# All matmul operands of a graph-attention kernel as f16 pairs, and four tiles a group transposed by DMA

## The reference

```
h = max(layernorm(x), 0)
q, k, v = h Wq^T, h Wk^T, h Wv^T + bv          (12 heads of 32)
p = softmax(q k^T * 384^-0.5 + 2 adj)           (rows of zeros give 0)
x = x + (p v) Wo^T + bo

h = max(layernorm(x), 0)
for l in 0, 1:
    u_left, u_right = h (h W_left^T)^T, h (h W_right^T)^T   (both / sqrt(384))
    e = exp(u_left above and on adj's diagonal, u_right below) * adj
    h = relu(norm(e / (sum e + 1e-10) (h W_lin^T + b_lin)) * ln_a + ln_b)
x = x + h
```

## Time and profile before

| | |
|---|---|
| median of 3 runs | 1509.78 us (1506.74 to 1509.90) |
| profiled execution | 1507.34 us, its span 1505.4 us |
| mean granted TensorE clock | 0.977 of 2.4 GHz |
| PE busy | 1432.3 us, 95% of the span, 14464 matmuls |
| DVE busy | 1243.8 us, 83% |
| ACT busy | 903.5 us, 60% |
| POOL busy | 508.9 us, 34% |
| HBM | 23.86 MB read, 12.58 MB written |

### The profile page before, as it was taken

One profiled execution on the slowest core, in us unless ns is written; L12 is line 12 of the kernel. 1 busy time (PEld: TensorE's weight loads), 2 busy tenths in 40 slices (PEclk: granted clock), 3 DMA queues, 4 the chain that ended last, 5 costly groups with the idle time before them and its releaser, 6 DMA issues.

```text
span 1505.4 us, 40241 instructions
## 1 busy us (share of the span) xinstructions
PE 1432.3 (95%) x14464; PEld 1396.4 (93%) x14464; DVE 1243.8 (83%) x4619; ACT 903.5 (60%) x2027; POOL 508.9 (34%) x921
## 2 busy tenths in 40 slices
PE   3699999999999999999999999999999999999874
PEld 3599999999999999999999999999999999999874
DVE  5578988888888888888888888888888888888853
ACT  4566665656666556666565666656666665566531
POOL 4113333233334233343323333333333342333321
PEclk8799999999999999999999999999999999999996
DMA  6232322223221223232222333222223222232200
GB/s 216 54 57 58 68 42 62 48 64 68 57 62 43 55 60 64 58 67 50 55 50 61 68 57 68 41 57 53 64 68 57 56 49 57 58 64 57 54 12 11
DMA packets 235683, 89.39 MB, mean 59 GB/s; under 512 B 206784, under 2 KB 235200, under 8 KB 235488
## 3 DMA queue, kind: packets, MB, share of 16 engines
q1 hardware_dynamic: 234912, 85.63, 26.9%
q0 software_dynamic: 576, 1.18, 0.3%
HBM read 23.86 MB, written 12.58 MB: 24 GB/s over the span
## 4 chain that ended last, share of the span: by engine, by line
PE 92%; DVE 2%; DMA 2%; ACT 1%; issue 1%; POOL 1%; SPq 0%; DVEq 0%; POOLq 0%; ACTq 0%
PE bank L342 79%; PE bank L348 4%; PE bank L415 4%; PE bank L403 3%; PE bank L422 1%; DMA x_sb<-x 1%; DMA pT<-prob_parts 1%; PE bank L434 0%; ACT prob L507 0%; SPq L323 0%; DVE weights L570 0%; ACT xn L490 0%; DVE stats_ln L598 0%; ACT prob_parts L515 0%; ACT work L556 0%
## 5 line engine op out<-in xcount | busy, mean ns | idle before, releaser
L342 PE MATMUL bank<-h,weights 128*128 128x256 f32 x3456 | 425.1, 280 | 3.0 <-DVE h L750 3.0
L342 PEld LDWEIGHTS bank<-h,weights 128*128 128x128 f32 x3456 | 411.9, 190 | 3.8 <-issue 3.7
L507 ACT ACTIVATE prob<-prob,rmin 128x128 f32<-128x128 f32 x768 | 244.2, 393 | 3.4 <-DVE rmin L665 3.4
L342 PE MATMUL bank<-weights,h 128*128 128x384 f32 x1152 | 227.5, 342 | 0.0
L342 PE MATMUL bank<-hA,weights 128*128 128x256 f32 x1728 | 219.2, 283 | 1.4 <-DVE hA L585 1.4
L342 PEld LDWEIGHTS bank<-hA,weights 128*128 128x128 f32 x1728 | 212.1, 190 | 1.7 <-DVE hA L585 1.7
L342 PEld LDWEIGHTS bank<-weights,h 128*128 128x128 f32 x1152 | 194.3, 188 | 6.3
L483 ACT ACTIVATE n<-bank 128x512 fp32r<-128x512 f32 x192 | 113.7, 592 | 141.7 <-PE bank L342 141.0
L800 POOL TENSOR_SCALAR less_mean_gnn<-mv_gnn 128x2 f32<-128x2 f32 x64 | 32.9, 513 | 429.9 <-DVE mv_gnn L590 429.9
L665 DVE CUSTOM_DVE_ANT_0 prob<-bank,adj_sb 128x128 f32<-128x128 f32 x768 | 171.0, 286 | 0.2 <-issue 0.2
L585 DVE TENSOR_TENSOR n<-bank,n 128x512 fp32r<-128x512 f32 x192 | 128.9, 684 | 33.8 <-ACT n L483 28.9
(11 more groups left out here) (101 smaller groups left out, 2453.8 us busy)
## 6 DMA issues: line engine op xcount, KB each, us to landing
x_sb<-x SPq DMA_DIRECT2D x32, 384.0 KB, 3.2
out<-x SPq DMA_DIRECT2D x32, 384.0 KB, 2.7
adj_sb<-adj SPq DMA_DIRECT2D x32, 128.0 KB, 2.1
pT<-prob_parts SPq DMA_TRANSPOSE x256, 2.8
x<-w SPq DMA_DIRECT2D x3, 576.0 KB, 4.8
pT<-w SPq DMA_DIRECT2D x3, 576.0 KB, 6.6
prob<-w SPq DMA_DIRECT2D x2, 576.0 KB, 7.3
prob_parts<-w SPq DMA_DIRECT2D x2, 576.0 KB, 6.0
```

What stands on the lines that cost most here:

```text
L342: mm = pe.matmul(out, lhsT, rhs, start=(n == 0), stop=(n == len(pairs) - 1))
L507: e = act.activation(prob[:, a * C + h // HC, :], prob[:, a * C + h // HC, :], ACT.Exp, bias=rmin[:, j, h:h + 1], scale=-1.0)
```

## The change

Each engine's order and the assignment of banks are written anew; the offsets now go from -2 to +1 (before from -1 to +2). Beside that:

- The weights, `hA`, `h0`, `h1`, `oT` and `n2` are f16 pairs. The weights are multiplied by 64 (`W_SCALE`) before the split, and whoever reads the product from PSUM multiplies by 1/64. For VectorE's low parts this makes `scalar_tensor_tensor` of `tensor_tensor`. `dT` and `hl` stay F32R.
- T1a, T1b, OT0, OT1, T2a, T2b, HTa and HTb are gone (24 transposes). In their place come XA, XO, XB and XC: ScalarE copies the rows of the group to a high part, 128 x 768 in f16, VectorE makes the low part, and SP transposes each of the two by one DMA: eight more DMA transposes a group.
- ln_a and ln_b of layer 0 are now applied to rows, by GpSimd (zc0, zc1, zd0, zd1: four operations of 128 x 384), and ScalarE's relu is in the high part of XC.
- `n2`, `hl`, `dT`, `c_sb` exist once for each layer, `mask` and `adjT` once for each of two groups, and layer 0's rows have a tile of their own (`xn2`).
- Seven of the ten weight matrices are staged at once (before four); the other three follow after the step tal.

```diff
-        W = sb("weights", [P, NW, 2, C, H], F32R)
+        W = sb("weights", [P, NW, 2, C, H], F16)
-        hA = sb("hA", [P, 2, C, T], F32R)
+        xa = sb("xn1_parts", [P, 2, G * H], F16)
+        hA = sb("hA", [P, 2, 2, G * C, P], F16)
-        h0 = sb("h0", [P, 2, C, T], F32R)
-        h1 = sb("h1", [P, 2, C, T], F32R)
-        n2 = sb("n2", [P, 2, 2, C, T], F32R)
+        h0 = sb("h0", [P, 2, 2, G * C, P], F16)
+        h1 = sb("h1", [P, 2, 2, G * C, P], F16)
+        n2 = sb("n2", [P, L, 2, 2, C, T], F16)
...
+                elif step in ("tah", "tal", "toh", "tol", "tbh", "tbl", "tch", "tcl"):
+
+                    part, k = "hl".index(step[2]), "X" + step[1].upper()
+                    sp.wait_ge(s_xparts[k][part], g + 1)
+                    for job in USERS[k]:
+                        wait_filled(sp, job, g - 2)
+                    src, dst = {"XA": (xa, hA), "XO": (xo, oT), "XB": (xb, h0), "XC": (xc, h1)}[k]
+                    sp.dma_start_transpose(dst[:, p, part, :, :], src[:, part, :]).then_inc(s_xturned[k][part], 16)
...
-                if step in ("T1a", "T1b"):
-                    for j in range(G):
-                        pe.wait_ge(s_xn1[j], g + 1)
-                    transposes(step, xn1, {"T1a": (0, 1), "T1b": (2,)}[step])
...
+            def split(k, g, rows_in, parts):
+                act.activation(parts[:, HI, :], rows_in.rearrange("p g h -> p (g h)"), ACT.Copy).then_inc(s_xparts[k][HI], 1)
...
+            def split(k, g, rows_in, parts):
+                dve.wait_ge(s_xparts[k][HI], g + 1)
+                ge(dve, s_xturned[k][LO], 16 * g)
+                dve.tensor_tensor(parts[:, LO, :], rows_in.rearrange("p g h -> p (g h)"), parts[:, HI, :], ALU.subtract).then_inc(s_xparts[k][LO], 1)
...
-                dve.tensor_tensor(out, src, hi_part if hi_part.dtype == F16 else hi_part.bitcast(F32), ALU.subtract).then_inc(free(job), 1)
+                dve.scalar_tensor_tensor(out=out, in0=src, scalar=W_BACK, in1=hi_part if hi_part.dtype == F16 else hi_part.bitcast(F32),
+                                         op0=ALU.mult, op1=ALU.subtract).then_inc(free(job), 1)
...
+                elif step[:2] == "zc":
+                    j = int(step[2])
+                    pool.wait_ge(s_z0[j], g + 1)
+                    pool.tensor_tensor(c_sb[:, 0, j, :], c_sb[:, 0, j, :], lna_all[:, 0, :], ALU.mult).then_inc(s_ca[j], 1)
```

SP's order after the change:

```
+        ("tch", -2), ("tcl", -2), ("ld_x", 1), ("pth00", 0), ("tbh", -1), ("tbl", -1), ("pth01", 0), ("ptl01", 0), ("ptl00", 0),
+        ("ld_adj", 1), ("tah", 1), ("tal", 1), ("pth10", 0), ("ptl10", 0), ("pth11", 0), ("ptl11", 0), ("out", -2), ("toh", 0),
+        ("tol", 0)],
```

More of the change, by code:

```diff
@@ L186, in build @@
         wu = work[:, 2 * T:3 * T].rearrange("p (g i) -> p g i", g=G)
[L187 to L191, removed]
+        dT = sb("dT", [P, L, 2, G, P], F32R)
+        c_sb = sb("c_sb", [P, L, G, H])
+        mask = sb("mask", [P, 2, G, 2, P])
+        adjT = sb("adjT", [P, 2, G, P])
         norms = ("ln1", "ln2", "gnn")
@@ L205, in build @@
         carrier = sb("carrier", [P, 4 + G * HC])
-        s_wload = [sem(f"weight_in{i}") for i in range(4)]
+        s_wload = [sem(f"weight_in{i}") for i in range(7)]
         s_setup, s_carrier = sem("setup"), sem("carrier")
@@ L331, in _ @@
                 if g == 0 and step == "ld_x":
-                    load_weights(range(4))
-                if g == 0 and step == "ld_adj":
-                    load_weights(range(4, NW))
+                    load_weights(range(7))
+                if g == 0 and step == "tal":
+                    load_weights(range(7, NW))
             for p in range(2):
@@ L343, in split_mm @@
                 return mm
-            def transposes(job, src, chunks):
-                for n, c in enumerate(chunks):
-                    for j in range(G):
-                        mm = pe.transpose(bank(job)[:, n * T + j * P:n * T + (j + 1) * P], src[:, j, c * P:(c + 1) * P], ident[:, :])
-                mm.then_inc(full(job), 1)
             def need(m, g):
@@ L417, in run @@
                     mm.then_inc(full(step), 1)
-                elif step[:2] == "OT":
-                    j = int(step[2])
-                    wait_drained(pe, f"PV{j}", g)
-                    for c in range(C):
-                        mm = pe.transpose(bank(step)[:, c * P:(c + 1) * P], o_sb[:, j, c * P:(c + 1) * P], ident[:, :])
-                    mm.then_inc(full(step), 1)
-                elif step[:2] == "WO":
-                    wait_drained(pe, f"OT{step[2]}", g)
-                    rows(step, g, WO, oT, 0)
-                elif step in ("T2a", "T2b"):
-                    for j in range(G):
-                        pe.wait_ge(s_xn2[j], g + 1)
-                    transposes(step, o_sb, {"T2a": (0, 1), "T2b": (2,)}[step])
+                elif step[:2] == "WO":
+                    wait_turned(pe, "XO", g)
+                    rows(step, g, WO, oT, int(step[2]))
                 elif step == "AT":
@@ L457, in run @@
                     if g == 0 and l == 0:
-                        pe.wait_ge(s_const, 1)
+                        pe.wait_ge(s_const, L)
                     pe.wait_ge(s_dlo[l], g + 1)
                     wait_drained(pe, f"HL{l}{j}", g)
-                    split_mm(bank(step)[:, 0:HL], [(dT[:, a, j, :], hl[:, b, j, :]) for a, b in PARTS]).then_inc(full(step), 1)
-                elif step in ("HTa", "HTb"):
-                    for j in range(G):
-                        pe.wait_ge(s_z0[j], g + 1)
-                    transposes(step, c_sb, {"HTa": (0, 1), "HTb": (2,)}[step])
+                    split_mm(bank(step)[:, 0:HL], [(dT[:, l, a, j, :], hl[:, l, b, j, :]) for a, b in PARTS]).then_inc(full(step), 1)
             pe.wait_ge(s_gconst, 1)
@@ L515, in run @@
                     act.activation(pp[:, HI, hs, :], prob[:, hs, :], ACT.Copy).then_inc(s_part[HI][b], 1)
-                elif step[:2] == "OT":
-                    j = int(step[2])
-                    hi(step, g, oT[:, HI, :, :], H, "p (c q) -> p c q", c=C)
+                elif step == "XO":
+                    for j in range(G):
+                        wait_drained(act, f"PV{j}", g)
+                    ge(act, s_xturned[step][HI], 16 * g)
+                    split(step, g, o_sb, xo)
                 elif step[:4] == "xn2_":
@@ L543, in run @@
                     act.wait_ge(s_gn[0], g + 1)
-                    act.activation(c_sb[:, j, :], c_sb[:, j, :], ACT.Identity, bias=shift["gnn"][:, j:j + 1],
+                    act.activation(c_sb[:, 0, j, :], c_sb[:, 0, j, :], ACT.Identity, bias=shift["gnn"][:, j:j + 1],
                                    scale=scale["gnn"][:, j:j + 1]).then_inc(s_z0[j], 1)
+                elif step == "XC":
+                    for j in range(G):
+                        act.wait_ge(s_cb[j], g + 1)
+                    ge(act, s_xturned[step][HI], 16 * g)
+                    act.activation(xc[:, HI, :], c_sb[:, 0, :, :].rearrange("p g h -> p (g h)"), ACT.Relu).then_inc(s_xparts[step][HI], 1)
                 elif step[:3] == "z1_":
@@ L623, in run @@
                     dve.wait_ge(s_dsum[l][j], g + 1)
-                    dve.scalar_tensor_tensor(out=c_sb[:, j, :], in0=bl_all[:, l, :], scalar=dsum[:, j:j + 1], in1=bank(job)[:, 0:H],
+                    dve.scalar_tensor_tensor(out=c_sb[:, l, j, :], in0=bl_all[:, l, :], scalar=dsum[:, j:j + 1], in1=bank(job)[:, 0:H],
                                              op0=ALU.mult, op1=ALU.add).then_inc(free(job), 1)
@@ L634, in run @@
                     aggregate("gnn").then_inc(s_gag[l], 1)
-                elif step == "T1a":
-                    lo(step, g, hA[:, LO, 0:2, :], hA[:, HI, 0:2, :], 2 * T, "p (c t) -> p c t", c=2)
-                elif step == "T1b":
-                    lo(step, g, hA[:, LO, 2, :], hA[:, HI, 2, :], T)
+                elif step in ("XA", "XO", "XB"):
+                    rows_in, parts = {"XA": (xn1, xa), "XO": (o_sb, xo), "XB": (xn2, xb)}[step]
+                    split(step, g, rows_in, parts)
+                elif step == "XC":
+                    dve.wait_ge(s_xparts[step][HI], g + 1)
+                    ge(dve, s_xturned[step][LO], 16 * g)
+                    dve.scalar_tensor_tensor(out=xc[:, LO, :], in0=c_sb[:, 0, :, :].rearrange("p g h -> p (g h)"), scalar=0.0, in1=xc[:, HI, :],
+                                             op0=ALU.max, op1=ALU.subtract).then_inc(s_xparts[step][LO], 1)
                 elif step[:2] == "QK":
@@ L653, in run @@
                     wait_filled(dve, job, g)
-                    dve.tensor_tensor(v_sum[:, j, :], bank(job)[:, 0:H], bv_all[:, :], ALU.add).then_inc(free(job), 1)
+                    dve.scalar_tensor_tensor(out=v_sum[:, j, :], in0=bank(job)[:, 0:H], scalar=W_BACK, in1=bv_all[:, :], op0=ALU.mult, op1=ALU.add).then_inc(free(job), 1)
                 elif step[0] == "S":
@@ L755, in _ @@
                     split_weights(SPLIT_AFTER["DVE"].get(step, ()))
```

(2 more changed lines are left out.)

210 lines of the change are left out of this document (101 added, 109 removed), and 38 rows, old and new, of the table ORDER.

## The result

The changed kernel takes 1535.76 us (median of 4 runs), beside 1508.62 us for the kernel before: a ratio of 1.0189, 95% interval 1.0153 to 1.0226. It is 1.9% slower; 1385 us was forecast. The profiled execution took 1537.1 us, its span is 1535.1 us. From one store of the result to the next, over 22 groups in the middle, a group takes 44.77 us (44.28 before, 40.1 forecast). 32 x 44.77 = 1433, so 104 us of the 1537.1 are filling and draining; 100 was forecast. Nearly the whole error is in the period: 4.7 us too little, 32 times.

What follows compares the result with a forecast made beforehand. TensorE's own work was taken as the bound: 32 x (39.8 us of work + 0.3 of waits) + 100 of filling and draining = 1383 us profiled, 1385 as a median. Forecast band 1335 to 1430 (0.62); 8-in-10 range 1335 to 1458.

Steps and rivals of the forecast that it cites:

- I take 0.3 us a period for such waits: Steady period: TensorE waiting for VectorE to release banks, as VectorE's slack falls from some 10 to 6 us.
- Filling and draining: First and last groups, where engines wait for each other: 92 us before, plus 8 net for longer hops, 100 us.
- the longer hop between the layers: End of layer 0's z0 to layer 1's start: 9.4 us in place of 4.2, counted in the draining.
- TensorE's work: Steady period: 24 transposes gone save 2.25 us, cheaper f16 matmuls 2.2, giving 39.8 us from 44.22.
- The sign that I gave for a failure: Whole kernel: the forecast fails above 1430 us if TensorE idles more than 1.5 us a period.
- I counted every matmul at 2.4 GHz: TensorE's matmuls: costs and floors of 107 and 160 ns assume the granted full clock.
- 38.4: TensorE's period in us by the skill's N/2.4 + 2.5 ns formula, some 45 us less time; not used in the sum.
- The hop through DMA: Transposes issued by SP: 1.22 us each to issue, about 2.8 to land, overlapping; 21 of SP's 40 us, hidden.
- the rival on the slower side: SP's in-order queue: transposes land one after another, 53 us a period, 1796 us; chance 0.07.
- order or VectorE paces it: Step order or VectorE, slowed by collisions with GpSimd, sets a 42.5 us period: 1460 us, range 1430 to 1500; chance 0.14.

Runs made afterwards that it cites:

- e1: Kernel before with its own orders and TensorE transposes; only weights, hA, h0, h1, oT and n2 made f16, without the factor 64: 1464.08 us, ratio 0.9704.
- e5: Changed kernel plus one unread GpSimd operation ahead of the layer-1 norm's arithmetic, on the suspected chain: 1617.41 us, 1.0716 of the kernel before.
- e6: Changed kernel plus the same unread GpSimd operation as e5, put behind zd0, off the suspected chain: 1549.60 us, 1.0260 of the kernel before.
- e4: Changed kernel with only the high parts of the four row tiles transposed by DMA, matmuls reading them for the low parts: 1501.52 us, ratio 0.9958.
- e9: Changed kernel with the result's store (out) moved behind transposes toh and tol in SP's order: 1526.91 us, 1.0128 of the kernel before.
- e10: Changed kernel with the store moved behind toh and tol, and zc and zd left out: 1508.44 us, 1.0010 of the kernel before.
- e7: e1 with only the hop between the layers done by DMA, without ln_a and ln_b of layer 0: 1569.42 us, 1.0405 of the kernel before.
- e8: e1 with only the hop of xn1 (first LayerNorm to QK) done by DMA: 1543.10 us, 1.0221 of the kernel before.
- e16: Changed kernel with unread matmuls filling TensorE's gaps, 12 ahead of S in a free bank, 8 ahead of WO: 1521.47 us, 1.0084 of the kernel before.
- e3: Changed kernel without zc and zd (ln_a and ln_b of layer 0 not applied): 1529.63 us, 1.0144 of the kernel before.
- e17: e9 with unread matmuls filling TensorE's gaps, 12 ahead of S in a free bank, 3 ahead of WO: 1514.88 us, 1.0044 of the kernel before.
- e2: Changed kernel with QK computed from the high parts alone, 12 of 18 matmuls left out in each of three jobs: 1540.12 us, ratio 1.0212.

## Why the prediction was wrong

**The step that failed** is "I take 0.3 us a period for such waits", with the hops costed under "Filling and draining. Here each hop counts in full". I had the longer hop between the layers at 9.4 us in place of 4.2, it measured 8.9, and I let it hide in the steady state because each engine's work fits into 40 us. The waits came to 3.9 us a period, not 0.3. Of the 4.7 us that the period is longer than the forecast, 3.6 are these waits, 0.75 the slow WO stages and 0.3 TensorE's work. The sign that I gave for a failure (over 1430 us if TensorE idles more than 1.5 us a period) is the one that came; I had put 0.92 on a faster kernel. Work that fits says nothing of latency. With written orders, each engine's step waits for its neighbour in the list as well as for its data, and the steps close to rings that run from one group into the next. Before, TensorE with 44.22 us a period was busy all the time, so no ring was longer than its work. e1's period of 42.94 is 3 us above my 39.8, but 2.2 of these are the transposes that e1 still has; 0.7 us a period is idle time, so the old orders leave hardly more to gain while no hop is longer than before. e5 and e6 show the ring by what it does to one operation, e4, e9 and e10 by what comes back when it is made shorter, e7 and e8 by what one hop costs.

**The clock** failed with it. I counted every matmul at 2.4 GHz. Behind idle gaps of 0.9 to 1.9 us 16 of 32 WO stages ran partly at the 1.2 GHz level: some 14 us of the 150 by e16.

**TensorE's work** was right in its sum, in part by luck. In the windows it is 403.7 us for 9.9 periods, 40.8 each; the WO groups, 39.9 us at their two speeds against 32.5 for as many matmuls of V, take 0.75 of it, which leaves 40.1 for a forecast 39.8. But the sizes were nearer the floor than I took (163 and 109 ns, not 168 and 112); with them the forecast would have been 38.6, 1.5 us under what came. Some 0.5 us of that is in the jobs that didn't change (C, PV, S), whose ends no next job overlaps when a gap follows; the rest I can't place. The Trainium skill (TensorE: Matmul & The Clock Gate, Back-to-back issue gap) gives 162.5 and 109 ns for an isolated matmul, and this trace agrees with that formula. The prediction's "38.4" for the period by it was miscalculated as well: its own sum gives 38.6, some 37 us less than mine and not 45.

**The hop through DMA** was right in its parts. SP issues a transpose in 1.24 us, and landing has not slowed under nearly double load:

```profile
L337 SPq DMA_TRANSPOSE pT<-prob_parts x256: 1209/1236/2405, 50.8 to 1447.1; - x128
...
DMA to landing us min/median/max: 2.7/2.8/6.4
```

SP's queue isn't the ring by its throughput, as the rival on the slower side had it (it forecast 53 us a period). But its order is part of the ring: `out` ahead of toh cost 9 us (uncertain by about 6), and 21 with zc and zd gone (e10 against e3).

**VectorE** is no bound by its load: it is busy 86% of the stretch, prob_parts takes 958 ns, 942 before, and e6 puts what 58 us more of GpSimd work cost at 14 us. The rival "order or VectorE paces it" named the right half, the order; but it was priced at 42.5 us a period by VectorE's load, had 0.14, and its 1430 to 1500 us don't hold the result either. TensorE's longest wait, S for VectorE's reading of QK1 (16.4 of 38.9 us), stands behind VectorE's list from PV1 on; no run made that list shorter.

**Filling and draining** came to 104 us, 100 forecast.

What stays open: which chain holds e17 at 44.0 us. Its gaps are filled, its store is out of the way, and zc and zd remain; e10 says that they are part of it, and e17's longest wait is N10's for the rows of that very hop (500 to 942.6 us):

```profile
PE bank L364 <- DMA h<-z_parts: 8.8, 10, 1.1
```

The remaining 4 us over the forecast I put down to the hops as in e7 and e8, but no run took all four back one at a time within the changed orders, and none has the new orders and banks with TensorE's transposes. So how much of the 72 us is the hops and how much the orders is not shown.

## What to carry to other kernels

When an engine is busy 100% of the steady state, its relief is worth only the distance to the next ring: before you price a saving, walk one turn of each chain that crosses into the next group (data, list neighbours and queue neighbours alike) and add up its latency; a hop that replaces a short on-chip step by a DMA adds the whole difference in latency to that sum. Put one small operation on the suspected chain and the same one off it: the difference tells a ring from a load. Once the busiest engine has gaps, look at its clock behind each gap before reading anything into a saving of work.

## What the hardware showed beyond that

- Behind gaps of 0.9 to 3 us TensorE's next stage ran partly at the 1.2 GHz level in some of the groups, not in all: WO took 3.08 or up to 4.77 us behind the same 1.0 us. Taking TensorE work away made it worse: 26 of 32 groups in e2.
- Twice the DMA transposes and a DMA share of 0.48 in place of 0.28 left the median landing of a pT transpose at 2.8 us.
